# Attention contexts kept with features on partitions, two heads added into the same rows, and row sums split between ScalarE and VectorE

## The chip, the cores and the metric
The kernel runs on one NeuronCore of a Trainium2 chip: TensorE (PE, with its weight loads as PEld), VectorE (DVE), ScalarE (ACT), GpSimd (POOL) and SyncE (SP, which here only issues transfers). The metric is the device time of one launch in microseconds (us); smaller is better.

## The reference
A language-model block over 64 sequences of 128 tokens, width 256, all in fp32:

```
x  = emb[wrapped and clipped ids]                         # 64 x 128 x 256
q, k, v = x Wq' + bq, x Wk' + bk, x Wv' + bv              # 16 heads of 16 features
attn = softmax(q k' / 4);  h = (attn v) Wo' + bo
n  = layernorm(h);  s = (n B') C'                         # state mixer
h  = h + sigmoid(n G' + g) * exclusive_scan(decay, s)     # over the 128 tokens
h  = h + layernorm(h) sign(F)'
```

## The kernel before
Two sequences make a pair; there are 32 pairs. A pair passes through the engines in a software pipeline: turn t does the scores and the softmax of pair t, the embedding, k and q of pair t+1, the rest of the context and the output projection of pair t-1, the first normalisation, gate and state products of pair t-2, the running sums over tokens and the second normalisation of pair t-3, and the last product and the store of pair t-4. Every engine has its own list of work of a turn, written out by hand in `turn(t, par)`; the engines meet only at semaphores. A wait written as `await_event(engine, semaphore, per, pair, nth)` waits until the semaphore has been raised nth times for this pair.

The softmax of a pair has eight steps s: step s takes sequence s // 4 and the four heads of group s % 4. PE first turns the probabilities of two steps ago (`turn_probs`, four 128x128 transposes into the bank ps_t), then makes the scores of step s (`scores`, into ps_s). DVE takes the row maxima (`maxima`, L506), ACT the exponentials of the four heads (`exponentials`, L368) and then moves the turned probabilities to SBUF (`move_probsT`, L377). Between the steps PE has its dense products. Of those, products that must be near fp32 run as three fp32r products of high and low parts: ACT rounds a block to its high part, DVE subtracts for the low part (`low_features`, `split_low`).

The context of a head is values times probabilities. v_aug holds per head 16 values, a column of ones and zeros up to 32 columns, so each head's product gives 32 rows of ps_c: 16 features, the row sum, and 15 rows of zeros. Four heads lie beside each other on 128 partitions, four groups fill the bank, one bank for each of the two sequences. These are fp32 products, which the trace shows as two instructions each. From there the context goes this way, per sequence b: ACT moves ps_c to ctx_raw (`move_ctx`, L383); PE turns it to tokens on partitions (`context_rows`, L732); DVE takes the reciprocal of the sums and multiplies (`context_norm`, L540 and L543) into ctx_tok. PE turns ctx_tok of both sequences back to features on partitions (`to_features`, L683), ACT rounds it to ctxT's high part (`move_block`, L390), DVE makes the low part (L514), and PE projects with wo. The four general banks g0 to g3 are handed round between all products of a turn; `await_first` names the reader that has to be done before a bank is written again. POOL gathers embeddings by an indirect transfer and does the element-wise parts of both normalisations, h1, and the high and low parts of the state. SP moves k and q into the stacks k_stack and q_stack for the scores, and stores y.

Of the kernel before, what the change touches and what calls it, by code (L numbers as in the profile page):

```python
# [29 lines left out]
fp32 = mybir.dt.float32  # L30
# [8 lines left out]
HEADS = 16  # L39
# [8 lines left out]
VW = 32  # L48
EPS = 1e-5
# [3 lines left out]
def build(nc, x, emb, wqT, bq, wkT, bk, wvT, bv, woT, bo, b_w, c_wT, gate_wT, gate_b, log_decay, ffn_wT, out):  # L53
    ctx = ExitStack()
    with ctx:  # L55
# [28 lines left out]
        bv_row, bo_row = sb("bv_row", [P, D]), sb("bo_row", [P, D])  # L84
# [17 lines left out]
        v_aug = [sb(f"v_aug{p}", [P, 2, HEADS, VW]) for p in range(2)]  # L102
# [3 lines left out]
        ctx_raw = [sb(f"ctx_raw{b}", [P, 4, SEQ]) for b in range(2)]  # L106
        inv_sum = sb("inv_sum", [P, 2, HEADS])
        ctx_tok = sb("ctx_tok", [P, 2, D])
# [42 lines left out]
        pe_ctxrow, pe_ctxT, pe_o, pe_xn1T = sem("pe_ctxrow"), sem("pe_ctxT"), sem("pe_o"), sem("pe_xn1T")  # L151
# [3 lines left out]
        act_x, act_exp, act_pT, act_ctx = sem("act_x"), sem("act_exp"), sem("act_pT"), sem("act_ctx")  # L155
# [10 lines left out]
        dve_ctxlo = sem("dve_ctxlo")  # L166
        dve_klo, dve_qlo, dve_xlo, dve_xn1lo, dve_xn2lo = (sem("dve_klo"), sem("dve_qlo"), sem("dve_xlo"),
# [85 lines left out]
        def _(pool):  # L253
# [46 lines left out]
            def turn(t, par):  # L300
                if exists(t - 3):
# [7 lines left out]
                                            ALU.subtract).then_inc(state_lows, 1)  # L309
                if exists(t - 2):  # L310
                    await_event(pool, dve_ve1, 1, t - 2, 1)
                    normalise(t - 2, t - 3, h0[par], mv1, ve1, rs1, xn1, pe_xn1T, centred1, rs1_done, pool_xn1)
                copy_ids(t + 2, par)
# [7 lines left out]
                gather(t + 2, par)  # L321
# [8 lines left out]
        def _(act):  # L330
            for n, (dst, src) in enumerate(((bq_raw, bq), (bk_col, bk), (ld_col, log_decay))):
                act.dma_start(dst[:], src).then_inc(small_loaded, 16)
            act.dma_start(bv_row[:], bv.partition_broadcast(P)).then_inc(small_loaded, 16)
# [13 lines left out]
            act.wait_ge(small_loaded, 96)  # L347
# [12 lines left out]
            def turn(t, par):  # L360
                def exponentials(s):

                    if exists(t):
                        await_event(act, dve_max, STEPS, t, s + 1)
                        p2, s2 = before(t, s, 2)
                        await_event(act, pe_pT, STEPS, p2, s2 + 1)
                        for j in range(HPS):
                            last = nc.scalar.activation(probs[s % 2][:, j], ps_s[s % 2][:, j * SEQ:j * SEQ + SEQ],  # L368
                                                        ACT.Exp, bias=neg_max[s % 2][:, j:j + 1])
                        last.then_inc(act_exp, 1)  # L370

                def move_probsT(s):
                    pair, st = before(t, s, 2)
                    if exists(pair):
                        await_event(act, pe_pT, STEPS, pair, st + 1)
                        await_event(act, pe_pv, STEPS, pair - 1, st + 1)
# [472 lines left out]
```

## Time and profile before

| | us |
|---|---|
| median of 3 runs (740.86 to 743.76) | 743.41 |
| the profiled execution | 738.42 |
| its span, first to last instruction | 736.4 |
| PE busy in the span | 685.7 |
| PEld busy | 644.1 |
| ACT busy | 575.5 |
| DVE busy | 531.3 |
| POOL busy | 377.2 |

The profiled execution is one launch; its span leaves out some 2 us around the first and last instruction. Busy time counts an engine's overlapping instructions once. An engine that starts its next instruction before the end of the last is measured better by the distance of two starts than by the duration of one. The mean granted clock of TensorE over the span was 0.973 of full speed.

### The profile page before, as it was taken

Reading aid. Unit: us, or ns where it says so; the run is one execution under the profiler, and the core shown is the slowest. Engines: PE = TensorE matmul, PEld = TensorE weight load, DVE = VectorE, ACT = ScalarE, POOL = GpSimd, SP = SyncE. Lnnn points to the kernel's source line nnn. Section 1 sums busy time; section 2 is a strip of 40 time slices with the busy share of each in tenths; the row PEclk is TensorE's granted clock in tenths of the full one; section 3 lists DMA queues with packets and bytes.
Section 4 is the critical chain, followed back from the end, with each engine's and each line's share of the span. In section 5 each row is a group of like instructions: output and inputs, shape, how many; then the busy total and the mean of one; then the engine's idle time right before and its main releaser. Section 6 shows DMA issues by size and latency. Waiting matters only on the chain. (4 is left out here: it accounts for less than half of the span.)

```text
span 736.4 us, 21129 instructions
## 1 busy us (share of the span) xinstructions
PE 685.7 (93%) x6983; PEld 644.1 (87%) x6983; DVE 531.3 (72%) x1175; ACT 575.5 (78%) x1641; POOL 377.2 (51%) x431
## 2 busy tenths in 40 slices
PE   3579999999999999999999999999999999999863
PEld 3477999998999999999999999999999999998752
DVE  3546677787778777787777777877787777877542
ACT  2478888887888888888888888888888888888410
POOL 7401355554565555554655555555655555554553
PEclk9799999999999999999999999999999999999985
DMA  5322333322333333223233333223333333221000
GB/s 142 112 91 87 102 101 116 110 82 85 88 112 114 108 105 114 100 73 92 91 114 114 100 114 110 97 76 89 97 114 114 100 114 107 89 82 66 16 14 28
DMA packets 56015, 69.66 MB, mean 95 GB/s; under 512 B 6768, under 2 KB 41648, under 8 KB 55984
## 3 DMA queue, kind: packets, MB, share of 16 engines
q1 hardware_dynamic: 52048, 60.48, 24.1%
q0 software_dynamic: 3072, 8.39, 6.2%
q10 hardware_dynamic: 864, 0.40, 0.2%
q8 instruction: 17, 0.28, 0.2%
q14 instruction: 14, 0.11, 0.1%
HBM read 10.52 MB, written 8.39 MB: 26 GB/s over the span
## 5 line engine op out<-in xcount | busy, mean ns | idle before, releaser
L368 ACT ACTIVATE probs<-ps_s,neg_max 128x128 f32<-128x128 f32 x1024 | 295.3, 384 | 79.1 <-DVE neg_max L506 79.1
L506 DVE TENSOR_REDUCE neg_max<-ps_s 128x4 f32<-128x512 f32 x256 | 175.8, 687 | 93.5 <-PE ps_s L634 93.2
L292 POOL TENSOR_TENSOR xn<-h,mv 128x512 f32<-128x512 f32 x64 | 66.6, 1040 | 220.7 <-DVE ve L533 220.7
L377 ACT COPY probsT<-ps_t 128x512 f32<-128x512 f32 x256 | 157.3, 614 | 11.4 <-PE ps_t L706 6.5
L706 PE MATMUL ps_t<-ident,probs 128*128 128x128 f32 x1024 | 154.8, 274 | 6.0 <-ACT probsT L377 5.7
L706 PEld LDWEIGHTS ps_t<-ident,probs 128*128 128x128 f32 x1024 | 120.5, 141 | 12.4 <-issue 4.6
L634 PE MATMUL ps_s<-k_stack,q_stack 128*128 128x256 f32 x512 | 124.7, 326 | 6.5 <-DMA q_stack<-q_low 6.5
L634 PEld LDWEIGHTS ps_s<-k_stack,q_stack 128*128 128x128 f32 x512 | 78.3, 194 | 7.2 <-DMA q_stack<-q_low 7.2
L285 POOL DMA_INDIRECT x_emb<-in_emb,id_col x64 | 65.4, 1022 | 23.3 <-issue 14.2
L521 DVE BATCH_NORM_STATS2 stats<-h 128x6 f32<-128x256 f32 x128 | 48.2, 419 | 33.7 <-POOL h L317 32.6
L297 POOL TENSOR_TENSOR xn<-xn,rs 128x512 f32<-128x512 f32 x64 | 66.6, 1041 | 9.2
L305 POOL TENSOR_TENSOR state_high<-state_in,ones_col 128x512 fp32r<-128x512 f32 x32 | 33.2, 1036 | 74.4 <-DVE state_in L623 74.4
L634 PE MATMUL ps_c<-probsT,v_aug 128*32 128x128 f32 x2048 | 69.3, 276 | 0.0
L634 PEld LDWEIGHTS ps_c<-probsT,v_aug 128*32 128x32 f32 x2048 | 51.9, 109 | 8.8 <-issue 0.2
L317 POOL TENSOR_TENSOR h<-gated,h 128x512 f32<-128x512 f32 x32 | 41.5, 1296 | 17.7 <-DVE gated L589 17.7
L383 ACT COPY ctx_raw<-ps_c 128x512 f32<-128x512 f32 x64 | 38.5, 602 | 13.9 <-PE ps_c L634 13.7
L683 PE MATMUL ps_g<-ident,xn 128*128 128x128 f32 x256 | 39.1, 276 | 9.6 <-POOL xn L297 9.6
L553 DVE SCALAR_TENSOR_TENSOR q_low<-ps_g,bq_col,q_high 128x256 fp32r<-128x256 f32 x64 | 28.0, 480 | 27.3 <-ACT q_high L423 27.3
L294 POOL TENSOR_TENSOR rs<-ve,neg_half 128x2 f32<-128x2 f32 x64 | 45.4, 710 | 0.0
L634 PE MATMUL ps_g<-wgh,xn1Th 128*128 128x256 f32 x128 | 40.4, 315 | 2.4 <-DVE xn1Tl L514 2.1
L308 POOL TENSOR_TENSOR state_low<-state_in,state_high 128x512 fp32r<-128x512 f32 x32 | 41.1, 1284 | 2.5
L634 PE MATMUL ps_g<-wsh,xn1Th 128*128 128x256 f32 x128 | 39.8, 311 | 0.0
(120 smaller groups left out, 1872.1 us busy)
## 6 DMA issues: line engine op xcount, KB each, us to landing
k_stack<-k_high SPq DMA_DIRECT2D x128, 128.0 KB
q_stack<-q_high SPq DMA_DIRECT2D x64, 256.0 KB
k_stack<-k_low SPq DMA_DIRECT2D x64, 128.0 KB
q_stack<-q_low SPq DMA_DIRECT2D x32, 256.0 KB
out<-y SPq DMA_DIRECT2D x32, 256.0 KB, 2.1
x_emb<-in_emb,id_col POOLq DMA_INDIRECT x64, 3.8
raw<-in_wkT SPq DMA_DIRECT2D x1, 256.0 KB, 3.1
raw<-in_wqT SPq DMA_DIRECT2D x1, 256.0 KB, 4.5
```

The source lines that it names most:

```text
L285: nc.gpsimd.indirect_dma_start(x_emb[par][b][:], None, emb, bass.IndirectOffsetOnAxis(ap=id_col[par][b][:], axis=0)).then_inc(gathered[par ...
L292: nc.gpsimd.tensor_tensor(xn[:], h[:], mv[:, :, 0:1].to_broadcast([P, 2, D]), ALU.subtract).then_inc(centred, 1)
L294: nc.gpsimd.tensor_tensor(rs[:], ve[:], neg_half[:], ALU.pow).then_inc(rs_done, 1)
L297: nc.gpsimd.tensor_tensor(xn[:], xn[:], rs[:].unsqueeze(2).to_broadcast([P, 2, D]), ALU.mult).then_inc(done, 1)
L308: nc.gpsimd.tensor_tensor(state_low[:], state_in[:], state_high[:].bitcast(fp32), ALU.subtract).then_inc(state_lows, 1)
L317: nc.gpsimd.tensor_tensor(h1[:], gated[:], h0[1 - par][:], ALU.add).then_inc(pool_h1, 1)
L368: last = nc.scalar.activation(probs[s % 2][:, j], ps_s[s % 2][:, j * SEQ:j * SEQ + SEQ], ACT.Exp, bias=neg_max[s % 2][:, j:j + 1])
L377: nc.scalar.copy(probsT[st][:], ps_t[:]).then_inc(act_pT, 1)
L506: nc.vector.tensor_reduce(neg_max[s % 2][:], ps_s[s % 2][:].rearrange("p (h k) -> p h k", h=HPS), axis=AX.X, op=ALU.max, negate=True).then ...
L521: nc.vector.bn_stats(stats[:, b], h[:, b]).then_inc(done_st, 1)
L634: return nc.tensor.matmul(dst, lhsT, rhs, start=first, stop=last)
L706: last = nc.tensor.transpose(ps_t[:, j * SEQ:j * SEQ + SEQ], probs[st % 2][:, j], ident[:])
```

## The change
The context stays with features on partitions all the way. v_wide holds for each head 32 columns in which only 16 are values: the first 16 for heads 0 to 7, the last 16 for heads 8 to 15. A head i of the first half and head i + 8 are added into the same 32 rows of ps_c (`context`, two products per place, the second accumulating), so both sequences and all sixteen heads fill one bank, and no row is empty. The rows of wo are put into that order on the host.

The row sums no longer come from a column of ones. ACT's exponential gives them as a second output (accum_out) in steps 0, 1, 2, 6 and 7; in steps 3, 4 and 5 (SUMMED) DVE adds up probs (`sums`). DVE takes the reciprocals of all 32 sums of a row in one operation (`invert_sums`), POOL spreads each over 16 columns (inv_wide), PE turns that to features on partitions (`invert_rows`, four transposes), ACT moves it to SBUF (`move_inverse`), DVE multiplies it with ps_c (`normalise_context`), ACT rounds the product to ctxT's high part (`move_ctx`), and DVE subtracts for the low part, now from ctx_feat in SBUF instead of from PSUM. `context_rows`, `context_norm` and the turning of ctx_tok are gone.

The order of a turn changes on every engine but SP; the diff shows only the places of the new work. POOL copies ids first and gathers right after the state parts. ACT moves probsT 6 ahead of exponentials 5, and xn2T and the probsT 7 ahead of the tanh. On DVE y comes behind the moments, v behind maximum 3, k_low behind maximum 4, and gate_in and state_in ahead of maximum 7. On PE the embedding's turning and the running sums come between scores 2 and the context. Cut to its core:

```diff
+HALF = HEADS // 2
+VROW = HD + HALF * VW
+SUMMED = (3, 4, 5)
...
+        v_wide = [sb(f"v_wide{p}", [P, 2, 2, VROW]) for p in range(2)]
+        row_sum = [sb(f"row_sum{p}", [P, 2, HEADS]) for p in range(2)]
...
+        inv_sum, inv_wide = sb("inv_sum", [P, 2, HALF, 2]), sb("inv_wide", [P, 2 * HEADS, HD])
+        inv_rows, ctx_feat = sb("inv_rows", [P, C * 2 * SEQ]), sb("ctx_feat", [P, C, 2, SEQ])
...
+                    await_event(pool, dve_inv, 1, t - 1, 1)
+                    await_event(pool, pe_inv, 1, t - 2, 1)
+                    nc.gpsimd.tensor_tensor(
+                        inv_wide[:], inv_sum[:].rearrange("p b i a -> p (b i a)").unsqueeze(2).to_broadcast([P, 2 * HEADS, HD]),
+                        ones_col[:, 0:1].unsqueeze(1).to_broadcast([P, 2 * HEADS, HD]), ALU.mult).then_inc(pool_inv, 1)
...
+                        if s - 2 in SUMMED:
+                            await_event(act, dve_sum, len(SUMMED), t, s - 2 - SUMMED[0] + 1)
                         for j in range(HPS):
+                            at = s % 4 * HPS + j
+                            taken = None if s in SUMMED else row_sum[par][:, s // 4, at:at + 1]
                             last = nc.scalar.activation(probs[s % 2][:, j], ps_s[s % 2][:, j * SEQ:j * SEQ + SEQ],
+                                                        ACT.Exp, bias=neg_max[s % 2][:, j:j + 1], accum_out=taken)
                         last.then_inc(act_exp, 1)
                 def move_probsT(s):
                     pair, st = before(t, s, 2)
                     if exists(pair):
                         await_event(act, pe_pT, STEPS, pair, st + 1)
+                        await_event(act, pe_pv, 2, pair - 1, st // 4 + 1)
                         nc.scalar.copy(probsT[st][:], ps_t[:]).then_inc(act_pT, 1)
+                def move_inverse(pair):
                     if exists(pair):
+                        await_event(act, pe_inv, 1, pair, 1)
+                        await_event(act, dve_ctx, 1, pair - 1, 1)
+                        nc.scalar.copy(inv_rows[:], g2[:]).then_inc(act_inv, 1)
+                def move_ctx(pair):
+                    if exists(pair):
+                        await_event(act, dve_ctx, 1, pair, 1)
+                        await_event(act, pe_o, 1, pair - 1, 1)
+                        nc.scalar.copy(ctxT[0][:], ctx_feat[:]).then_inc(act_ctxT, 1)
...
+                move_probsT(4)
                 move_block(t - 2, xn1T[0], g3, pe_xn1T, pe_state, act_xn1T)
-                move_probsT(4)
                 exponentials(4)
+                move_inverse(t - 1)
                 move_probsT(5)
...
+                move_ctx(t - 1)
+                move_probsT(6)
                 exponentials(5)
-                move_probsT(6)
                 exponentials(6)
...
+                def sums(s):
+                    if exists(t):
+                        await_event(dve, act_exp, STEPS, t, s + 1)
+                        nc.vector.tensor_reduce(row_sum[par][:, s // 4, s % 4 * HPS:s % 4 * HPS + HPS], probs[s % 2][:],
+                                                axis=AX.X, op=ALU.add).then_inc(dve_sum, 1)
+                def invert_sums():
                     if exists(t - 1):
+                        await_event(dve, act_exp, STEPS, t - 1, STEPS)
+                        await_event(dve, dve_sum, len(SUMMED), t - 1, len(SUMMED))
+                        await_event(dve, pool_inv, 1, t - 2, 1)
+                        nc.vector.reciprocal(inv_sum[:].rearrange("p b i a -> p b a i"),
+                                             row_sum[1 - par][:].rearrange("p b (a i) -> p b a i", a=2)).then_inc(dve_inv, 1)
+                def normalise_context():
+                    if exists(t - 1):
+                        await_event(dve, pe_pv, 2, t - 1, 2)
+                        await_event(dve, act_inv, 1, t - 1, 1)
+                        await_event(dve, dve_ctxlo, 1, t - 2, 1)
+                        nc.vector.tensor_tensor(ctx_feat[:].rearrange("p c b s -> p (c b s)"), ps_c[:], inv_rows[:],
                                                 ALU.mult).then_inc(dve_ctx, 1)
...
                 low_features(t - 2, xn1T, g3, act_xn1T, pe_state, dve_xn1lo)
...
+                sums(3)
+                normalise_context()
...
                 maxima(5)
...
+                sums(4)
...
                 maxima(6)
...
+                    await_event(dve, act_ctxT, 1, t - 1, 1)
+                    await_event(dve, pe_o, 1, t - 2, 1)
+                    nc.vector.tensor_tensor(ctxT[1][:], ctx_feat[:], ctxT[0][:].bitcast(fp32),
+                                            ALU.subtract).then_inc(dve_ctxlo, 1)
+                sums(5)
...
+                def context(b, pair, vp):
+                    if not exists(pair):
+                        return
+                    await_event(pe, act_pT, STEPS, pair, 4 * b + 4)
+                    if b == 0:
+                        await_event(pe, dve_v, 1, pair, 1)
+                        await_event(pe, dve_ctx, 1, pair - 1, 1)
+                    for c in range(C):
+                        at = slice((2 * c + b) * SEQ, (2 * c + b + 1) * SEQ)
+                        for a in range(2):
+                            for j in range(4):
+                                i = 4 * c + j
+                                head = HALF * a + i
+                                values = v_wide[vp][:, b, a, HD - HD * a + VW * i:HD - HD * a + VW * i + VW]
+                                last = mm(ps_c[VW * j:VW * j + VW, at], values,
+                                          probsT[head // HPS + 4 * b][:, head % HPS], a == 0, a == 1)
+                    last.then_inc(pe_pv, 1)
+                def invert_rows(dst):
+                    await_event(pe, pool_inv, 1, t - 1, 1)
+                    for c in range(C):
+                        for b in range(2):
+                            at = (2 * c + b) * SEQ
+                            last = nc.tensor.transpose(
+                                dst[:, at:at + SEQ],
+                                inv_wide[:, HEADS * b + HALF * c:HEADS * b + HALF * c + HALF].rearrange("p h d -> p (h d)"),
+                                ident[:])
+                    last.then_inc(pe_inv, 1)
...
                 attention(4)
...
+                    invert_rows(g2)
...
                 attention(6)
+                context(b=0, pair=t, vp=par)
```

Further lines rename v_aug, bv_row and their semaphores, load bv twice so that it has a row for either sequence, and count the prologue's semaphores anew. `move_probsT` waits for the context of its whole sequence, since that raises its semaphore once now.

## Rows read from the trace of the kernel before

**Rows 1.** The head of the page: the span, then busy time of each engine.

```profile
span 736.4 us, 21129 instructions
...
PE 685.7 (93%) x6983; PEld 644.1 (87%) x6983; DVE 531.3 (72%) x1175; ACT 575.5 (78%) x1641; POOL 377.2 (51%) x431
```

**Rows 2.** Busy time by stretch: its length, each engine, clock, DMA share.

```profile
170.00:666.00 496.00, 495.74 (x5210) 470.47 (x5211) 388.12 (x861) 423.82 (x1217) 269.54 (x307) 1.00 0.33 101
```

**Rows 3.** Timeline of L567 (start, duration), once in a turn.

```profile
150.57 0.67 DVE L567 TENSOR_TENSOR y<-ps_g,h 128x512 f32<-128x512 f32 x1
...
671.04 0.68 DVE L567 TENSOR_TENSOR y<-ps_g,h 128x512 f32<-128x512 f32 x1
```

**Rows 4.** All waits of PE, 150 to 670 us: total, times, longest.

```profile
PE ps_s L634 <- DMA q_stack<-q_low: 1.1, 1, 1.1
```

**Rows 5.** Timeline of all engines, 400 to 404 us (start, duration).

```profile
400.05 0.60 PE L732 MATMUL ps_g<-ident,ctx_raw 128*128 128x128 f32 x4
...
400.49 0.60 PE L706 MATMUL ps_t<-ident,probs 128*128 128x128 f32 x4
...
401.16 0.28 PE L634 MATMUL ps_g<-wvh,xTh 128*128 128x256 f32 x1
...
401.20 0.59 ACT L377 COPY probsT<-ps_t 128x512 f32<-128x512 f32 x1
...
402.60 0.60 PE L683 MATMUL ps_g<-ident,x_emb 128*128 128x128 f32 x4
...
403.04 0.60 PE L706 MATMUL ps_t<-ident,probs 128*128 128x128 f32 x4
...
403.39 0.48 PE L634 MATMUL ps_s<-k_stack,q_stack 128*128 128x256 f32 x2
...
403.80 1.08 PE L634 MATMUL ps_c<-probsT,v_aug 128*32 128x128 f32 x32
...
403.91 0.69 DVE L506 TENSOR_REDUCE neg_max<-ps_s 128x4 f32<-128x512 f32 x1 [0.42 <-PE ps_s L634]
```

**Rows 6.** Groups of ACT: count, busy us, mean ns, idle before.

```profile
L368 ACT ACTIVATE probs<-ps_s,neg_max 128x128 f32<-128x128 f32 x1024 | 295.3, 384 | 79.1 <-DVE neg_max L506 79.1
L377 ACT COPY probsT<-ps_t 128x512 f32<-128x512 f32 x256 | 157.3, 614 | 11.4 <-PE ps_t L706 6.5
...
L383 ACT COPY ctx_raw<-ps_c 128x512 f32<-128x512 f32 x64 | 38.5, 602 | 13.9 <-PE ps_c L634 13.7
...
L390 ACT CAST ctxTh<-ps_g 128x512 fp32r<-128x512 f32 x32 | 21.8, 680 | 2.5 <-PE ps_g L683 2.5
L434 ACT ACTIVATE gate_tanh<-gate_in 128x512 f32<-128x512 f32 x32 | 21.8, 680 | 7.9 <-DVE gate_in L615 7.9
```

**Rows 7.** Timeline of ACT (start, duration), in the prologue and in turns.

```profile
21.07 0.20 ACT L352 ACTIVATE e_ld<-ld_col 128x2 f32<-128x2 f32 x1
21.16 0.61 ACT L339 CAST wgh<-raw 128x512 fp32r<-128x512 f32 x1
...
431.71 1.14 ACT L368 ACTIVATE probs<-ps_s,neg_max 128x128 f32<-128x128 f32 x4 [1.17 <-DVE neg_max L506]
432.73 0.60 ACT L377 COPY probsT<-ps_t 128x512 f32<-128x512 f32 x1
433.19 0.88 ACT L423 ACTIVATE q_high<-ps_g,bq_col 128x256 fp32r<-128x256 f32 x2
433.91 1.19 ACT L368 ACTIVATE probs<-ps_s,neg_max 128x128 f32<-128x128 f32 x4
```

**Rows 8.** Groups of DVE, columns as in rows 6.

```profile
L506 DVE TENSOR_REDUCE neg_max<-ps_s 128x4 f32<-128x512 f32 x256 | 175.8, 687 | 93.5 <-PE ps_s L634 93.2
...
L543 DVE TENSOR_TENSOR ctx_tok<-ps_g,inv_sum 128x256 f32<-128x256 f32 x64 | 27.2, 424 | 2.2
...
L540 DVE RECIPROCAL inv_sum<-ps_g 128x16 f32<-128x16 f32 x64 | 16.4, 257 | 7.4 <-PE ps_g L732 3.2 <-DVE stats L521 2.3
```

**Rows 9.** A group of POOL, columns as in rows 6.

```profile
L305 POOL TENSOR_TENSOR state_high<-state_in,ones_col 128x512 fp32r<-128x512 f32 x32 | 33.2, 1036 | 74.4 <-DVE state_in L623 74.4
```

More of the change, by code:

```diff
@@ L309, in turn @@
                                             ALU.subtract).then_inc(state_lows, 1)
+                gather(t + 2, par)
                 if exists(t - 2):
@@ L447, in _ @@
             for par in range(2):
[L448 removed]
+                nc.vector.memset(v_wide[par][:], 0.0).then_inc(prep_step, 1)
             dve.wait_ge(prep_step, 4)
[L450 to L451 removed]
             dve.wait_ge(x_loaded, 16)
@@ L563, in turn @@
                     norm_stats(t - 2, h0[par], dve_h0, stats1, dve_st1)
+                if exists(t - 2):
+                    await_stats(t - 2, dve_st1, pool_xn1)
+                maxima(1)
+                if exists(t - 2):
+                    norm_moments(stats1, mv1, ve1, dve_mv1, dve_ve1, t - 2)
                 if exists(t - 4):
@@ L616, in turn @@
                                             gb_row[:].unsqueeze(1).to_broadcast([P, 2, D]), ALU.add).then_inc(dve_gate, 1)
-                low_features(t - 1, ctxT, g2, act_ctxT, pe_o, dve_ctxlo)
-                maxima(7)
                 if exists(t - 2):
@@ L625, in turn @@
                                             ALU.mult).then_inc(dve_in, 1)
+                maxima(7)
                 low_features(t - 3, xn2T, g3, act_xn2T, pe_ffn, dve_xn2lo)
@@ L707, in turn_probs @@
                     last.then_inc(pe_pT, 1)
-                def context(s):
-                    for back in (6, 5, 4, 3):
-                        pair, st = before(t, s, back)
-                        if not exists(pair):
-                            continue
-                        vp = par if s >= back else 1 - par
-                        b, g = divmod(st, 4)
-                        await_event(pe, act_pT, STEPS, pair, st + 1)
-                        if st == 0:
-                            await_event(pe, dve_v, 1, pair, 1)
-                            await_event(pe, act_ctx, 2, pair - 1, 2)
-                        if st == 4:
-                            await_event(pe, act_ctx, 2, pair, 1)
-                        for j in range(HPS):
-                            last = mm(ps_c[VW * j:VW * j + VW, g * SEQ:g * SEQ + SEQ],
-                                      v_aug[vp][:, b, g * HPS + j], probsT[st][:, j])
-                        last.then_inc(pe_pv, 1)
@@ L728, in context_rows @@
-                def context_rows(b, dst):
-                    await_event(pe, act_ctx, 2, t - 1, b + 1)
-                    for g in range(4):
-                        last = nc.tensor.transpose(dst[:, g * P:g * P + P], ctx_raw[b][:, g], ident[:])
-                    last.then_inc(pe_ctxrow, 1)
+                def context(b, pair, vp):
[15 more added lines that the diff above has]
+                    last.then_inc(pe_pv, 1)
@@ new lines, in invert_rows @@
+                def invert_rows(dst):
+                    await_event(pe, pool_inv, 1, t - 1, 1)
+                    for c in range(C):
+                        for b in range(2):
+                            at = (2 * c + b) * SEQ
[4 more added lines that the diff above has]
+                    last.then_inc(pe_inv, 1)
@@ L773, in turn @@
                     mm(g0[:], earlier[:], state_low[:].rearrange("p b d -> p (b d)"), False, True).then_inc(pe_sums, 1)
+                context(b=1, pair=t - 1, vp=1 - par)
                 attention(3)
```

111 lines of the change are left out of this document (38 added, 73 removed).

## The prediction, made before the run
> **What bounds the kernel now.** I read the head of the page first, then the busy time of the steady stretch, then the starts of one instruction that comes once a turn, then the waits, and last the order of time within one turn. The reader is to see this. PE and PEld head the page [rows 1]. In the 496 us between 170 and 666 us PE is busy for all but 0.3 us at a granted clock of 1.00, which is its upper level, 2.4 GHz; ACT has 423.8 us, DVE 388.1 us and POOL 269.5 us [rows 2]. The write of y comes once a turn; its starts at 150.57 and 671.04 us are pairs 2 and 27, so 25 turns take 520.47 us, **20.82 us a turn** [rows 3]. Over nearly the same stretch the list of what PE waited for has a single entry, 1.1 us for a stack transfer [rows 4]. Busy alone would not prove a bound, since matmul spans overlap; that nothing is waited for and that starts follow each other at a fixed step does. Two starts show the step: a block of four 128x128 fp32 transposes, begun at 402.60 us, lets the next begin 0.44 us later, and a group of twelve 128x256 matmuls 1.44 us later (401.16 to 402.60) [rows 5]. So PE's own queue sets the turn, and each block taken out is worth its spacing, until another engine is full. Per turn (496 us are 23.8 turns) the others have ACT 17.8, DVE 16.3, POOL 11.3 us of busy time.
>
> **The change on PE.** Removed per pair: two context_rows (four transposes each) and the four of ctx_tok, three blocks. Added: invert_rows, one block of the same form. The context_rows block starts at 400.05, the next block at 400.49: 0.44 us [rows 5]. The other two forms share shape and type, so I price them equal. Net 2 x 0.44 = **0.88 us a turn**. The context products stay 16 fp32 products a batch, 32 columns wide, rotating over the four column places as before; that two heads now add in the same rows changes which flag they carry, not count or size. Bounds for this: the zero half of the operands costs nothing by itself; an accumulating product could cost more than an overwriting one, but the trace has accumulating products of the wide form at the same 1.44 us for twelve, so I take nothing, and at most a doubling of one 32-product block, 1.08 us [rows 5], which I do not believe. Moving context(b=1) behind the token transposes and the running sums changes no amount.
>
> The new turn is 20.82 - 0.88 = 19.94 us if PE stays the bound. The blocks run in turns 1 to 32. Turn 32 lies behind the last scores, where latencies count and not amounts, so I take 31 turns: 31 x 0.88 = **27.3 us**.
>
> **The change on ACT, the disputed part.** Removed: two moves of ctx_raw, 0.60 us each, and the move of ctxTh from PSUM, 0.68. Added: the move of inv_rows from PSUM, like ctx_raw, 0.60, and the cast of ctx_feat from SBUF, nearest row the tanh, SBUF to SBUF, 0.68 [rows 6]. Net -0.6 us. ACT's instructions overlap, so what counts when it is full is the step between starts: four exponentials 1.02 us (431.71 to 432.73), a probsT move 0.46 (to 433.19), the two halves of q_high 0.72 (to 433.91) [rows 7]. A turn after the change then is 8 x 1.02 + 8 x 0.46 + 2 x 0.72 + about 6 x 0.5 (xT, xn1T, xn2T, ctxT, inv_rows, tanh) = 16.3 us.
>
> To this come 20 row sums a turn (five steps of four heads) as an output of the exponential, which the trace of before doesn't show. Bound below: nothing, if the sum rides in the instruction; it can't be a gain, since the same exponentials remain. Nearest rows for a readout of its own: the smallest ACTIVATE, 128x2, lasts 0.20 us and lets the next start after 0.09 [rows 7]. Bound above: the readout waits for its exponential to end (0.384 us long, 0.255 between starts, so 0.13 of overlap is lost [rows 6, 7]) and stands by itself for 0.20: 0.33 each. Times 20 that is 0, 1.8 or 6.6 us: ACT 16.3, 18.1 or 22.9 us. I take 0.10 each, 2.0 us and 18.3 us in all, since this engine's instructions all overlap their neighbours in the rows. ACT meets PE's 19.94 at (19.94 - 16.3)/20 = 0.18 us each, and the old turn of 20.82 at 0.23.
>
> The Trainium skill (ScalarE: Activation LUTs, What ACT_TABLE_LOAD costs) gives an ACTIVATE with immediate operands 186 ns plus its elements, with about 93 ns of overlap with its neighbour. By it, if a readout is such an instruction, 20 of them are 1.9 us with the overlap and 3.7 us without, which would put ACT at 18.2 or 20.0 us; it prices no readout, and no run yet shows one. Its figure for an exponential of 128 with a pointer bias, 387 ns, agrees with the 384 of the trace.
>
> **DVE.** Removed: two reciprocals of 16 columns (16.4/32 = 0.51 us a turn) and two products of 256 (27.2/32 = 0.85) [rows 8]. Added: one reciprocal of 32 columns (0.26 to 0.30), one 512-wide product (0.68), and three sums over 128x512, priced as the maxima, 0.69 each; they read SBUF and not PSUM, and I let the same row bound them on both sides. Net +1.7, so 18.0 us of busy time, 90% of the new turn. It fits. **POOL.** inv_wide is a 128x512 product like state_high, 1.04 us [rows 9]: 12.3 us of 19.94. It stands behind h1 and ahead of the second normalisation. The gather moves ahead of both normalisations; its rows are wanted a turn later.
>
> **Does the order hold?** I laid the new queues on PE's clock, in us from the first transpose of a turn, with blocks of 0.44, 1.44 and about 1.0 (context) and 0.35 for the transposes of a step when its scores follow [rows 5]. Steps begin at 0, 1.8, 3.9, 6.7, 8.8, 11.8, 13.9 and 17.7, and the next turn at 19.9. A probsT move starts 0.71 after its transposes; a maximum starts 0.52 after its scores and takes 0.69 [rows 5]. With 1.42 us for a step that reads sums out, exponentials end at 3.0, 4.9, 7.3, 9.3, 12.0, 16.2, 17.6 and 20.9; PE wants them at 3.9, 6.7, 8.8, 11.8, 13.9, 17.7, 19.9 and 21.7. The wait put in new on DVE, normalise_context for inv_rows, has maximum 5, q_low and the sum of step 4 queued behind it: inv_rows lands at 12.6, DVE gets there at 12.7. ACT's move of probsT 6 now stands ahead of exponentials 5 and waits for PE to 14.7; exponentials 5 are ready by 16.2 where 17.7 is wanted. invert_rows, at 9.9, wants inv_wide, which follows gated (6.5), h1 (to 8.2) and its own 1.04: 9.4. The out projection wants ctxTl at 18.4 and has it at 16.5. q_low comes two DVE operations later in the queue, but three groups of twelve matmuls and a context stand between it and the next scores, and before only one such wait of 1.1 us is seen [rows 4]. The tight place is the turn's seam: exponentials 7, then the move of probsT 0, ready 0.15 us before PE's step 1. From a readout of about 0.13 us on, this begins to stall PE, by what 20 readouts are dearer.
>
> So all edits but the readouts, the sums and the two blocks are costed at nothing, and PE's queue is what hides them; where it drains they cost their stall.
>
> **The sum.** The profiled execution took 738.4 us (span 736.4 and 2.0 around it); 738.4 - 27.3 = 711.1. The runs shown have a median of 743.4, 5.0 above the profiled one; I take the same difference off: **716 us**.
>
> **Rivals.**
> 1. *ACT becomes the bound* (the other side). If a readout neither overlaps its exponential nor its successor, ACT needs from 0.23 us each 20.9 us a turn and more; at 0.25 it is 21.3, +0.5 x 31 = +15: 759 us; at 0.33, 22.9: 808 us. It decides from 0.23 us each. For it: the rows hold no such instruction, and a sum can only be read when it is whole. Against it: the 0.09 us step behind the small ACTIVATE. Chance 0.14. At 186 ns each, the skill's figure without overlap, ACT's 20.0 us would just pass PE's 19.94, and the time be about 718 to 724.
> 2. *The new order stalls PE, faster but by less.* At 0.15 to 0.2 a readout, the seam costs 0.4 to 0.7 us of the 0.88. Or ctxlo, whose two inputs now both lie in SBUF, and a POOL product hold each other up: by at most POOL's 1.04 us [rows 9], of which about 0.4 is free before maximum 7; that delays exponentials 7 at the seam. With 0.4 us lost a turn, 743.4 - 31 x 0.48 = 728 us. Chance 0.13. The skill (SBUF — State Buffer, Who interferes with whom) says that a VectorE instruction with two SBUF inputs contends with a GpSimd one that reads SBUF; the rows of before show no VectorE operation of that kind in the steady stretch, so the trace neither bears it out nor denies it.
> 3. *Nothing measurable*: the same losses come to 0.75 to 1.0 us a turn, 740 to 747 us. Or the removed transposes had not been on the path; PE's one wait in 520 us speaks against that. Chance 0.06.
>
> The forecast itself, PE still the bound, has 0.67, with a range of its own of 709 to 722: below, the small bubbles beside the removed blocks go too (some 0.2 us a turn, 6 us); above, they grow by as much.
>
> **Numbers.** A measurement of this kernel tells about 0.5% (3.7 us) from no change. Faster: 0.67 + 0.13 = 0.80; the same 0.06; slower 0.14. The range runs from 709, below which I leave 0.05, through rivals 2 and 3's near side, to 742, above which I leave the 0.14 of rival 1 and a little of rival 3.
>
> **What the profile after would show.** y every 19.9 to 20.0 us and PE's wait list nearly empty: right. A readout row for ACT, 640 of them, with 0.09 to 0.12 us between its start and the next: the price right; exponentials of a summed step taking 1.4 us between starts. If PE waits for ACT's probs or probsT in every turn, rival 1 or 2 is on; waits at step 1 of PE mean the seam. DVE at 90% and no PE wait for ctxTl or inv_wide: the rest right. What would make me wrong is above all the readout's price, and next a POOL or DVE operation that is much dearer from SBUF than its row.

## The result and the profile after

| | before | after |
|---|---|---|
| median, range | 742.13 us (739.51 to 743.76) | **707.08 us** (706.2 to 708.52) |
| profiled execution, span | 738.4, 736.4 | 708.5, 706.8 |
| first y, y of 27 turns later, us | 109.1, 671.04 | 108.61, 644.98 |
| turn | 20.81 us | 19.87 us |

The ratio is 0.9533 (0.9497 to 0.9569): 35.0 us faster, where 27.3 were forecast, and 2 us below the range. Medians here and below leave out executions in which the granted clock was far lower than usual; there were two, both of the kernel before. The head of the page after, with the columns of [rows 1]:

```profile
span 706.8 us, 21274 instructions
...
PE 654.8 (93%) x6727; PEld 610.3 (86%) x6727; DVE 582.4 (82%) x1205; ACT 614.0 (87%) x2249; POOL 408.2 (58%) x463
```

PE has 256 products fewer: 8 transposes in each of 32 turns. DVE, ACT and POOL all have more busy time in a shorter span. The steady stretch, with the columns of [rows 2], and the first and last of 28 starts of y, as in [rows 3]:

```profile
170.00:640.00 470.00, 469.43 (x4982) 442.37 (x4973) 422.34 (x877) 449.46 (x1652) 288.34 (x325) 1.00 0.33 106
```

```profile
108.61 0.68 DVE L602 TENSOR_TENSOR y<-ps_g,h 128x512 f32<-128x512 f32 x1
...
644.98 0.69 DVE L602 TENSOR_TENSOR y<-ps_g,h 128x512 f32<-128x512 f32 x1
```

PE is busy for all but 0.6 of 470 us at the upper clock, and the list of its waits between 150 and 640 us, [rows 4] before, is empty. So PE sets the turn still, with ACT busy for 96% and DVE for 90% of the stretch. The groups of the page for the new work (count, busy us, mean ns, idle before):

```profile
L389 ACT ACTIVATE probs<-ps_s,neg_max 128x128 f32<-128x128 f32 x1024 | 339.4, 387 | 26.2 <-DVE neg_max L523 21.9
...
L389 ACT ACTIVATION_READ_ACCUMULATOR probs<-ps_s,neg_max 128x1 f32 x640 | 138.6, 217 | 0.0
...
L556 DVE TENSOR_REDUCE row_sum<-probs 128x4 f32<-128x512 f32 x96 | 65.2, 679 | 0.0
...
L332 POOL TENSOR_TENSOR inv_wide<-inv_sum,ones_col 128x512 f32<-128x512 f32 x32 | 33.3, 1040 | 18.5 <-DVE inv_sum L565 18.5
```

The readout is an instruction of its own, 640 of them, 217 ns long. What it costs is not its length but the step between starts, in the timeline of ACT:

```profile
404.20 0.37 ACT L389 ACTIVATE probs<-ps_s,neg_max 128x128 f32<-128x128 f32 x1
...
404.46 0.19 ACT L389 ACTIVATION_READ_ACCUMULATOR probs<-ps_s,neg_max 128x1 f32 x1
404.56 0.36 ACT L389 ACTIVATE probs<-ps_s,neg_max 128x128 f32<-128x128 f32 x1
...
404.81 0.20 ACT L389 ACTIVATION_READ_ACCUMULATOR probs<-ps_s,neg_max 128x1 f32 x1
404.90 0.37 ACT L389 ACTIVATE probs<-ps_s,neg_max 128x128 f32<-128x128 f32 x1
```

In these rows the readout starts 0.25 us after its exponential, the step that exponentials had without readouts [rows 7], and the next exponential starts 0.09 to 0.10 us after it. It overlaps with the instruction on either side of it, and its price is under half of the 0.23 us from which rival 1 decides.

**Where the 35 us are.** From span to span: up to the first y -0.5 us, 27 turns -25.6, behind them -3.5 (65.36 to 61.82), together -29.6. The other 5 us are not in these two profiles: before's profiled execution was 3.7 us below the median of its runs, after's 1.4 us above its own. Below, the experiments take PE's amount of work and the rest of the change apart.

### The profile page after: what moved, and what is told of

Same layout as the page of the kernel before. It is cut to its first block, busy times and chain, and to the rows that moved or that the text cites. A ratio compares the mean times of both kernels' runs of the same rounds, so it can differ in the third digit from the quotient of the medians.

```text
span 706.8 us, 21274 instructions
## 1 busy us (share of the span) xinstructions
PE 654.8 (93%) x6727; PEld 610.3 (86%) x6727; DVE 582.4 (82%) x1205; ACT 614.0 (87%) x2249; POOL 408.2 (58%) x463
## 4 chain that ended last, share of the span: by engine, by line
PE 83%; DVE 4%; ACT 3%; POOL 2%; issue 2%; SPq 2%; DMA 2%; POOLq 0%; DVEq 0%; ACTq 0%
PE ps_g L671 43%; PE ps_t L743 16%; PE ps_c L671 8%; PE ps_s L671 8%; PE ps_g L720 6%; ACT probs L389 2%; PE ps_g L772 2%; SPq L248 2%; DMA q_stack<-q_low 1%; DVE neg_max L523 1%; DMA x_emb<-in_emb,id_col 1%; DVE stats L538 1%; POOL h L327 1%; SPq L253 1%; POOL k_stack L339 1%
## 5 line engine op out<-in xcount | busy, mean ns | idle before, releaser
L389 ACT ACTIVATE probs<-ps_s,neg_max 128x128 f32<-128x128 f32 x1024 | 339.4, 387 | 26.2 <-DVE neg_max L523 21.9
L743 PE MATMUL ps_t<-ident,probs 128*128 128x128 f32 x1024 | 157.4, 276 | 6.7 <-ACT probsT L398 5.4
L389 ACT ACTIVATION_READ_ACCUMULATOR probs<-ps_s,neg_max 128x1 f32 x640 | 138.6, 217 | 0.0
L743 PEld LDWEIGHTS ps_t<-ident,probs 128*128 128x128 f32 x1024 | 115.8, 141 | 18.4 <-issue 11.1
L671 PE MATMUL ps_c<-probsT,v_wide 128*32 128x128 f32 x2048 | 69.2, 276 | 0.0
L671 PEld LDWEIGHTS ps_c<-probsT,v_wide 128*32 128x32 f32 x2048 | 52.0, 109 | 15.7 <-issue 11.1
L556 DVE TENSOR_REDUCE row_sum<-probs 128x4 f32<-128x512 f32 x96 | 65.2, 679 | 0.0
L332 POOL TENSOR_TENSOR inv_wide<-inv_sum,ones_col 128x512 f32<-128x512 f32 x32 | 33.3, 1040 | 18.5 <-DVE inv_sum L565 18.5
L417 ACT CAST xn2Th<-ps_g 128x512 fp32r<-128x512 f32 x32 | 18.8, 588 | 25.3 <-PE ps_g L720 24.1
```

Source lines behind the costliest of these rows:

```text
L556: nc.vector.tensor_reduce(row_sum[par][:, s // 4, s % 4 * HPS:s % 4 * HPS + HPS], probs[s % 2][:], axis=AX.X, op=ALU.add).then_inc(dve_sum, 1)
L671: return nc.tensor.matmul(dst, lhsT, rhs, start=first, stop=last)
L743: last = nc.tensor.transpose(ps_t[:, j * SEQ:j * SEQ + SEQ], probs[st % 2][:, j], ident[:])
```

## The experiments

All ratios are to the kernel before, run in between on the same chip; its median there, in us, is in brackets. In kernels that start from after, the line numbers are after's or one more; in those from before, before's or one more.

**1. The four corners: PE's amount, and the rest of the change.** Each kernel has PE's old or new amount of work, and the old or new form of all else. `b_again` is the kernel before unchanged.

> The kernel before, unchanged, as a control and as a second profile of it. The medians moved by 35.0 us, the two profiled executions by 29.9 (738.4 to 708.5); the other 5 us are the difference between the profiled execution of before and its median. If that execution was merely the low end of a spread, this one lies near 742 with the same turn of 20.81 us and the same end; if a profiled execution of before is always low, it is 738 again. Ratio to before 1.00 within 0.4%.

742.95 us [742.5], 1.0011 (0.9994 to 1.0027). Its profiled execution took 739.9 us; the turn in it is 21.05 us ((674.25 - 105.82)/27), not 20.81, and PE does wait:

```profile
PE ps_g L634 <- DVE xn2Tl L514: 2.5, 11, 0.3
```

In 170 to 640 us PE was busy 465.9 of 470 us, where the profile on which the prediction rests had 0.3 us idle in 496 [rows 2]. In that execution PE was kept waiting once [rows 4]; in this one it has 4 us of gaps and waits in every second turn for xn2Tl, the low part of the second normalisation.

The time of an execution also goes with its granted clock. Of the 23 of the kernel before on this chip, the seven with a mean granted clock of 0.971 took 743.5 to 745.3 us, the four at 0.973 took 742.4 to 743.4, and the two at 0.979 took 739.9 and 740.8. In the three profiles at hand the clock in the steady stretch was 1.00, the upper level of 2.4 GHz; they differ outside it, between 40 and 60 us for example, where it was 0.91 in before, 1.00 in b_again and 0.83 in after. So an execution can be placed only beside others of its clock. b_again's profiled one has the turn of 21.05 us and is yet the fastest of the 23: its clock is 0.979. The profiled execution of before, at 0.973, took 738.4 us, 4 to 5 less than these four (its chip may be another one), and its 27 turns were 6.5 us shorter than b_again's. PE's nearly empty wait list belongs to that execution.

`b_fewer`: the kernel before with eight transposes fewer a turn (the parts of the context that they would bring are missing from the result, so only the time is of use).

```
-                    for g in range(4):          # context_rows
+                    for g in range(1):
-                    to_features(g2, lambda b: ctx_tok[:, b], pe_ctxT)
+                    to_features(g2, lambda b: ctx_tok[:, b], pe_ctxT, blocks=1)
```

> The kernel before with eight transposes a turn left out of PE's list and nothing else changed (three of four in each context_rows, two of four of ctx_tok; that part of the context is left out of the result). Theory A, only PE's amount counts at its old spacing: 0.11 us x 8 = 0.88 us a turn, 742.1 - 27.3 = 714.8 us. Theory B, the change's new order and its shorter tail bring the remaining 7.7 of the 35.0 us: also 714.8 here, with the tail as long as before. Theory C, the blocks themselves cost more than their spacing, so that all 35 us come with them: 707.

733.09 us, 0.9882 (0.9859 to 0.9905): 9.4 us, a third of what the amount is worth. PE's waits, 150 to 640 us, and one of them in the timeline:

```profile
PE ps_g L634 <- DVE xn1Tl L514: 10.9, 24, 0.5
PE ps_g L634 <- DVE xn2Tl L514: 3.1, 12, 0.4
```

```profile
402.44 0.75 DVE L521 BATCH_NORM_STATS2 stats<-h 128x6 f32<-128x256 f32 x2 [0.87 <-POOL h L317]
...
405.33 0.68 DVE L514 TENSOR_TENSOR xn1Tl<-ps_g,xn1Th 128x512 fp32r<-128x512 f32 x1
...
406.14 0.38 PE L634 MATMUL ps_g<-wgh,xn1Th 128*128 128x256 f32 x1 [0.38 <-DVE xn1Tl L514]
```

In every turn the gate product waits for xn1Tl, the low part of the first normalisation. It stands in VectorE's queue behind the statistics of h1 (they wait 0.87 or 0.96 us for POOL), the second context_norm, k_low and maximum 4. The wait for POOL isn't new: it is in the profile of the kernel before, to the tenth the same as here and in b_again, and it is gone in after and in a_padded:

```profile
DVE stats L521 <- POOL h L317: 22.0, 24, 1.0
```

`a_padded`: the kernel after with the invert_rows block issued three times, so PE's amount is the old one.

```
-                    for c in range(C):          # invert_rows
+                    for again, c in ((n, c) for n in range(3) for c in range(C)):
```

> The changed kernel with its block of four transposes made three times, so that PE has the amount of before again; all other engines as after. Theories A and B: 707.1 + 27.3 = 734.4 us, and 7.7 us below before remain for order and tail. Theory C: 742. If PE were no longer the bound after the change (ACT or DVE instead), the added blocks would be partly hidden: below 730.

733.82 us, 0.9878 (0.9858 to 0.9899); turn 20.74 us, PE busy 469.4 of 470 us, no wait. So with PE's old amount the changed kernel is 8.7 us faster than before, and the two blocks are worth 733.8 - 707.1 = 26.7 us in it; the turn falls from 20.74 to 19.87 us, by 0.87, as priced. The 8.7 us are not the order alone: a_padded has all else of the change too, the row sums, the single bank, and no context_norm. All of that together is called the new form here. Later, on another chip [741.7], both once more as `a_ladder3` and `a_ladder4`:

> The kernel of a_padded again (new order, TensorE's old amount). If the order is worth the same on any chip: ratio 0.986 to 0.990. If the slower before of the other chips was what the order won back: 0.995 to 1.0 on a chip where before takes 735.

> The changed kernel again, unchanged: 26 to 27 us below a_ladder3 on any chip (two blocks, 31 times 0.43 to 0.44), and 705 to 708 us.

733.99 us, 0.9906 (0.9881 to 0.9932), and 708.03 us, 0.955 (0.9527 to 0.9573): 7.7 us for the new form, 26.0 for the amount. The corners are: old form 742.5 and 733.1, new form 733.8 and 707.1. Amount alone 9.4, form alone 8.7, both 35.4: half of the gain, 17 us, comes only with both.

**2. The readouts.** `a_again` is after unchanged; `a_noread` leaves the readouts out and keeps ones in row_sum, so that the probabilities of five steps are not divided by their sums.

```
-   taken = None if s in SUMMED else row_sum[par][:, s // 4, at:at + 1]
+   taken = None
```

> The changed kernel, unchanged, as the yardstick of this series: 707 us, 0.953 of before.

> The changed kernel without any sum read out on ACT (the sums of steps 0, 1, 2, 6 and 7 are left out of the result, ones stand in their place); all else as after. ACT has 1.8 us less a turn. If PE alone bounds the changed kernel: 707 again, within 1.5 us. If the turn's seam (exponentials 7, probsT 0, PE's step 1) still costs the 0.15 us a turn that stand before PE's step 1 in its trace: 707 - 27 x 0.15 = 703. If ACT is the true bound: 27 x 1.8 = 49 us less is possible at most, until PE's bare amount of about 19.3 us a turn: 692.

707.62 us [744.33], 0.9514 (0.9484 to 0.9544), and 706.75 us, 0.9502 (0.9479 to 0.9526): without 20 readouts a turn nothing measurable changes. `a_read32` adds twelve, in the steps that VectorE sums, into a tile that nobody reads:

```
-   taken = None if s in SUMMED else row_sum[par][:, s // 4, at:at + 1]
+   taken = unused_sum[:, at:at + 1] if s in SUMMED else row_sum[par][:, s // 4, at:at + 1]
```

> The changed kernel with the sum read out in all eight steps, the twelve new ones into a tile that nobody reads; DVE still sums three steps. ACT gets 12 x 0.09 = 1.1 us more a turn. If PE bounds and ACT has room (17.9 us by distances of starts, of 19.87): within 2 us of 707. If ACT is as good as full through its waits in order, each of those steps being 0.36 us later stalls PE: 0.3 to 1.1 us a turn, 716 to 741.

717.96 us [742.5], 0.9667 (0.9647 to 0.9687), and a wait that after doesn't have:

```profile
PE ps_t L744 <- ACT probsT L399: 6.0, 23, 0.3
```

Twelve more readouts are about 1.1 us of ACT a turn and cost 0.29 us of turn (20.16). This is the seam of the prediction: the wait is at PE's step 1 (309.85 us in this trace), for which the exponentials 7 (from 307.72) and the move of probsT 0 (309.11 to 309.71) come late. The expectation of the next run, which calls it the wait for probsT 3, is wrong there. `a_actonly` takes the sums away from VectorE altogether:

```
-SUMMED = (3, 4, 5)
+SUMMED = ()
...
-                sums(3)                 # and sums(4), sums(5)
```

> The changed kernel with all eight steps summed by ACT's readouts and none by DVE. ACT has 1.1 us a turn more, DVE 1.8 less. With the twelve readouts alone (DVE still summing) it was 718.0, PE waiting for probsT 3 in every turn. If that wait is made by ACT's queue alone: 717 to 719 again. If DVE's sums were part of the chain (they stand ahead of normalise_context and maxima 5 and 6): 708 to 714. If relieving DVE outweighs it: below 707.

715.46 us [743.0], 0.9645 (0.9607 to 0.9684), the same wait, 4.7 us. So the readouts of five steps fit under PE and those of eight do not; the split is worth some 8 us.

**3. One piece of the new order undone.** Both kernels keep the new path of the context. `a_old_sums`: the token transposes stand ahead of scores 2 again, the running sums (with gated) behind the context and xTl.

```
                     token_major(g2, wv, xT, PARTS, pe_v)
+                    to_features(g3, lambda b: x_emb[1 - par][b], pe_x)
                 attention(2)
-                    to_features(g3, lambda b: x_emb[1 - par][b], pe_x)
+                context(b=1, pair=t - 1, vp=1 - par)
                 # running sums into g0
-                context(b=1, pair=t - 1, vp=1 - par)
```

> The changed kernel with one piece of the old order: the embedding's transposes ahead of scores 2 and the running sums behind the context on PE, and on DVE gated behind xTl. Theory A (only PE's amount counts): 707. Theory D (the old order kept g and ffn waiting, through gated, h1, stats, k_low and xn1Tl on DVE, and the new order's gain of about 8 us comes from taking the sums and gated early): DVE idles before stats for POOL's h1 again, PE waits for xn1Tl before the gate product, 0.2 to 0.5 us a turn, 713 to 721.

716.92 us [744.33], 0.9644 (0.9619 to 0.9668). Not the wait that was expected (xn1Tl), but:

```profile
PE ps_g L772 <- POOL inv_wide L332: 5.2, 24, 0.3
```

```profile
417.20 0.63 PE L772 MATMUL ps_g<-ident,inv_wide 128*128 128x128 f32 x4 [0.16 <-POOL inv_wide L332]
```

`a_state_late`: state_in behind maximum 7, where before has it.

```
-                # state_in
                 maxima(7)
+                # state_in
```

> The changed kernel with state_in behind maximum 7 as of old. Theory E: xn2Tl is late for ffn again, and exponentials 7 gain 0; PE waits 0.2 to 0.4 us a turn, 713 to 718. If the changed kernel has room there through its other moves: 707.

720.88 us [743.0], 0.9715 (0.9684 to 0.9746); again

```profile
PE ps_g L772 <- POOL inv_wide L332: 6.6, 23, 0.4
```

POOL works in order: state_high waits 117.6 us in all for state_in between 150 and 640 us, where it waited 78.4 in after, so all behind it (the normalisation, h1, inv_wide) is late. The new chain (row sums, inverse, inv_wide, invert_rows) needs gated and state_in early; each piece undone costs 9 to 14 us. Since the kernel before has no such chain, these are prices of the new order for the new path, not what it would bring the old one.

**4. Which piece of the old order blocks?** `b_sums_first_fewer`: before with sums and gated first, and the eight transposes gone.

```
-                    if s in (2, 6):                    # TensorE
+                    if s == 6:
                         context(s)
                 # running sums into g0
+                context(2)
...
                 maxima(2)                              # VectorE
+                # gated
                 # v_aug, xTl
-                # gated
```

> The kernel before with the same eight transposes left out as in the second run (three of four in each context_rows, two of four of ctx_tok; that part is left out of the result), and with the running sums ahead of context(2) on PE and gated as the first product behind maximum 2 on DVE. Without the reorder it was 733.1, only 9.4 below before, since PE then waited 0.5 us a turn for xn1Tl. Theory D: that wait goes or shrinks, 715 to 725. If the wait has another cause (ACT's place for xn1Th, or k_low ahead of maximum 4): 731 to 734.

737.54 us [744.33], 0.9923 (0.9895 to 0.995), no faster than b_fewer (0.9882; the intervals meet). The wait went to the operation that was now queued behind gated:

```profile
PE ps_g L634 <- DVE xTl L514: 6.6, 24, 0.3
PE ps_g L634 <- DVE xn2Tl L514: 4.5, 18, 0.4
```

So the theory that gated's place makes the wait fell. `b_state_early` puts state_in ahead of maximum 7, `b_state_early_fewer` takes the transposes out too:

```
+                # state_in
                 maxima(7)
-                # state_in
```

> The kernel before with one DVE operation moved: state_in ahead of maximum 7 instead of behind it. Theory E: in its second profile (the control) PE idles 0.25 to 0.3 us before ffn in most turns, because xn2Tl comes behind scores 7, maximum 7 and state_in, 2.4 us after scores 7 begin, and PE needs it after 2.1; the control's turn is 21.05 us against 20.74 of the padded new kernel with the same PE amount. The move takes 0.6 us off this chain: turn 20.75 to 20.8, time 743 - 27 x 0.3 = 735. If the difference lies in other places of the order: 742.

> The same, with the eight transposes left out as before (three of four in each context_rows, two of four of ctx_tok; that part is left out of the result). Without the move it was 733.1. Its trace has two stalls a turn: 0.5 us before the gate product for xn1Tl, 0.2 to 0.3 before ffn for xn2Tl. Theory E: the second goes, the first stays, 726 to 729. If the eight blocks were only bounded by the ffn stall: 715.

738.99 us [743.0], 0.9955 (0.9934 to 0.9977), and 730.47 us, 0.9846 (0.9813 to 0.9879); as `b_ladder1` on another chip [741.7] 731.61 us, 0.9869 (0.9836 to 0.9902). State_in early gives about 4 us, between the two expectations; it is the one piece of the new order that was priced in the old form. The xn1Tl wait stays: 11.3 us, up to 0.7.

> The kernel of b_state_early_fewer again, on the chip of the next three. Ratio to before 0.985 if the earlier one (0.9846) holds on any chip.

`b_norm_late` and `b_norm_late_fewer` also move the second context_norm behind the moments of pair t-3, out of xn1Tl's way, and its transposes behind the gate product:

```
-                context_norm(1, g2)
                 if exists(t + 1):
                     split_low(k_low, g1, bk_col, k_high, act_khi, dve_klo)
...
                     norm_moments(stats2, mv2, ve2, dve_mv2, dve_ve2, t - 3)
+                context_norm(1, g2)
```

> The kernel before with state_in ahead of maximum 7, and the second context_norm moved behind the moments of pair t-3 on VectorE (with its ctx_tok transposes behind the gate product on TensorE). No amount changes. If context_norm ahead of xn1Tl holds up the gate product only when transposes are gone, this equals its parent: 737 to 740. If it costs part of a stall in the full kernel too: 734 to 736.

> The same with eight transposes fewer a turn (two context_rows blocks cut to one transpose each, ctx_tok to two). Theory (VectorE's queue ahead of xn1Tl makes PE wait 0.7 us at the gate product, and that stall takes the removed transposes' time): reciprocal and product, 0.6 us, leave the queue, so the turn falls from 20.66 by 0.5 to 0.6 us to about 20.1, 715 to 720 us. Rival (the wait moves to the next late thing, as it did with gated first: q_low, ctxTh or the seam): 726 to 731.

730.48 us [734.6], 0.9946 (0.9928 to 0.9965), and 715.97 us, 0.9745 (0.972 to 0.977). The amount is worth 14.5 us here, against 8.5 between the two kernels without the move, which ran on another chip. The profile of the second still has the wait, shorter than the 11.3 us above:

```profile
PE ps_g L635 <- DVE xn1Tl L514: 7.9, 24, 0.4
```

But before took 734.6 us on this chip, and 742.5, 743.0 and 744.3 on those of the earlier runs, so `b_ladder2` ran b_norm_late_fewer's kernel once more, beside b_ladder1.

> The kernel of b_norm_late_fewer again. If moving the second context_norm behind xn1Tl is what pays, it is 6 to 12 us below b_ladder1 on the same chip; if the difference between 730.5 and 716.0 was mostly the chip (before was 743.0 on the one, 734.6 on the other), 0 to 3 us.

750.58 us [741.7], 1.014 (1.0106 to 1.0175): outside both expectations, and 34.6 us above the same program on the other chip. The timeline of PE and ACT at the context product of the first sequence, in b_ladder2 and then in b_norm_late_fewer:

```profile
415.30 1.08 PE L635 MATMUL ps_c<-probsT,v_aug 128*32 128x128 f32 x32
...
415.76 0.68 ACT L390 CAST ctxTh<-ps_g 128x512 fp32r<-128x512 f32 x1
...
418.30 0.59 ACT L383 COPY ctx_raw<-ps_c 128x512 f32<-128x512 f32 x1 [1.86 <-remote]
```

```profile
403.40 1.08 PE L635 MATMUL ps_c<-probsT,v_aug 128*32 128x128 f32 x32
...
403.87 0.67 ACT L390 CAST ctxTh<-ps_g 128x512 fp32r<-128x512 f32 x1
...
404.63 0.59 ACT L383 COPY ctx_raw<-ps_c 128x512 f32<-128x512 f32 x1
```

The product that the move waits for ends 1.08 us after its start in both; the move starts 0.15 us later in the one, 1.92 us later in the other, and so in each of 23 turns (43.5 us in all). The profile names no engine as releaser ("remote"), and ACT has no such wait in any other run here. In both, ACT ends ctxTh within 0.1 us of the product's end. Why it goes on at once on one chip and not on the other stays open; no further run bears on it. So what moving context_norm is worth was measured only on one chip, and there by ratio to a faster before.

## Why the prediction missed

**PE sets the turn: right, of one execution.** The profile's turn was 20.81 us, the one of b_again 21.05, with PE waiting for xn2Tl. The near-empty list [rows 4] was taken for the kernel, and in b_again it isn't empty.

**Two blocks at 0.44 us, 31 times, 27.3 us: right, sized 1 us high.** 26.7 and 26.0 us in the new form. The forecast turn was 19.94 us, the measured one 19.87.

**The readout, 0.10 us: right.** It is 0.09 to 0.10 in the timeline, costs nothing measurable as placed, and the seam is where more of it starts to cost, as the prediction named. Rival 1 is refuted: at 20 a turn ACT isn't the bound. DVE, POOL and their new work: right, 0.68 and 1.04 us each; only the reciprocal is dearer, 0.34 us for 0.26 to 0.30.

**Rival 2's contention: real, but out of the way.** ctxTl, now with two inputs in SBUF, seems hardly dearer than xTl with one in PSUM:

```profile
L647 DVE TENSOR_TENSOR ctxTl<-ctx_feat,ctxTh 128x512 fp32r<-128x512 f32 x32 | 22.7, 710 | 0.7 <-ACT ctxTh L410 0.7
L531 DVE TENSOR_TENSOR xTl<-ps_g,xTh 128x512 fp32r<-128x512 f32 x32 | 22.1, 691 | 5.4 <-ACT xTh L417 5.4
```

The mean hides it. Of the 32 ctxTl, 30 run while POOL stands still and one beside the last 0.08 us of a product of POOL; all these take 0.68 us. The last one starts together with a product of POOL that reads SBUF:

```profile
670.25 1.04 POOL L306 TENSOR_TENSOR xn<-xn,rs 128x512 f32<-128x512 f32 x1
670.26 1.57 DVE L647 TENSOR_TENSOR ctxTl<-ctx_feat,ctxTh 128x512 fp32r<-128x512 f32 x1 [0.69 <-ACT ctxTh L410]
```

It takes 0.9 us longer, in a_again and a_ladder4 too, while POOL's product is no longer than usual. In a_read32 and a_old_sums the two overlap by 0.58 us, and it takes 1.12; in a_padded by 0.16, and it takes 0.70. xTl, with one input in PSUM, runs beside POOL in 31 of 32 turns and takes 0.69 us in each. The Trainium skill (SBUF — State Buffer, Who interferes with whom) says that a VectorE instruction with two SBUF inputs contends with a GpSimd one that reads SBUF; the trace agrees, by these 0.9 us for 1.03 us of overlap. The rival's bound of POOL's 1.04 us was right. What it would cost in every turn wasn't tried: in the steady turns the queues keep the two apart.

**The step that failed is "all edits but the readouts, the sums and the two blocks are costed at nothing".** That term was put at 0 us, and it measured 8.7 and 7.7: a_padded and a_ladder3 have those edits with PE's old amount. The sum can be read by medians, since taking "the same difference off" makes it 743.4 - 27.3 = 716. Against it, the edits at nothing brought 7.7 to 8.7 us more, the two blocks 0.6 to 1.3 less, and the kernel before measured 742.1 in place of 743.4. Together that is 7.7 to 9.4 us, where 9.0 are missing (716.1 - 707.1). The reason given for the nothing, that PE's queue hides them, held for the one execution of the profile, with a turn of 20.81 us; in b_again the turn is 21.05 and PE waits for xn2Tl, in a_padded it is 20.74 without a wait.

Of this term, state_in's place is about 4 us, by b_state_early. What the rest is stays open: other places in the order, or the new path. That context_norm no longer stands ahead of xn1Tl isn't it, as far as b_norm_late tells: with PE's old amount its move brought nothing measurable (0.9946, where b_state_early had 0.9955, on another chip). Part of the rest may lie behind the steady turns: from the last of the 28 starts of y to the end it took 65.4 and 63.9 us in the two profiles of before, 60.9 and 62.0 in those of the padded kernel.

Profile to profile the forecast was 738.4 - 27.3 = 711.1, and 708.5 was measured, only 2.6 less. The two gaps between profile and median, 5.0 us taken and -1.4 found, depend on which executions were profiled: before's was a fast one for its clock, and after's had the lowest clock of its four, 0.970, where the others had 0.976 and 0.977 and took 706.2 to 707.4 us.

**What the prediction didn't see at all:** that in the old form the two blocks would have brought 9.4 us. It priced amounts by PE's spacing "until another engine is full". No engine was full in b_fewer: PE waits, and DVE idles some 0.9 us for POOL in each turn. The account that fits is a chain through three engines (gated, h1, statistics, k_low, maximum 4, xn1Tl) that was as long as PE's queue between the running sums and the gate product. For it speak the wait itself and that it fell from up to 0.7 to up to 0.4 us when 0.68 us of work left it (0.26 and 0.42), though on another chip; that nothing else stands behind it isn't shown. A sign of the chain could be read before: the 22.0 us that DVE idles for POOL's h1 in the kernel before. In the new form the amount counts in full, and PE's list is empty in after and in a_padded.

## What to carry to other kernels

Work taken off a full engine that works in order is worth its spacing only if the chains through the other engines have as much slack as you take. The list of the full engine's waits doesn't tell, since it is empty also where they are just short enough. Look at the waits of the other engines instead, and follow one late operand back through each queue. Cut the amount and the rest of a change apart in experiments: pad the new kernel back to the old amount, and cut the amount in the old kernel. Before a profile's wait list is taken for the kernel's, profile it a second time, and compare an execution only with others of the same granted clock.

## What the runs showed of the hardware

- The readout of ScalarE's row sum is an instruction of 217 ns on average, and the next exponential starts 0.09 to 0.10 us after it; 32 instead of 20 of them a turn cost 11 us through a wait, 0 instead of 20 gained nothing measurable.
- A VectorE subtraction over 128x512 with both inputs in SBUF took 0.68 us alone, 1.12 us where it overlapped a GpSimd product that reads SBUF by 0.58 us, and 1.57 where by 1.03 us; with one input in PSUM it took 0.69 us beside GpSimd.
- The kernel before took 734.6 us on one chip and 741.7 to 744.3 on four others; after wasn't run on the first. Its three medians were 707.1, 707.6 and 708.0.
- On one chip, 23 executions of one program took from 745.3 us at a mean granted clock of 0.971 down to 739.9 at 0.979.
- One program took 715.97 us on one chip and 750.58 on another, with a 1.9 us wait a turn that the profile gives no releaser for.
